# A selective-scan and mixture kernel: its first two and last two steps get their own order of stages and the PSUM banks of the scans

## What is computed

```
x = x + block(layernorm(x));  x = x + experts(layernorm(x))
block(x):   u = layernorm(x)*w + b; xm, z = split(u @ in_proj)
            xc = silu(conv4(xm) + b);  low, B, C = split(xc @ x_proj)
            dt = softplus(low @ dt_proj + b)
            for t: h = h*exp(dt*A) + dt*B*xc;  y = sum_s(h*C)   # 16 states s, 512 channels
            x1 = x + ((y + xc*D) * silu(z)) @ out_proj
            x2 = x1 + (silu(gate) * up) @ ff_out, gate and up from layernorm(x1) @ ff_proj
experts(x): weights of the best 2 of softmax(x/|x| @ router);  sum_e w_e * (x @ Wa[e] @ Wb[e])
```

## Time and profile before

| | |
|---|---|
| median of 3 runs | 1402.63 (1399.36 to 1402.98) |
| profiled execution | 1402.94, span 1401.2 |
| TensorE matmul busy | 1246.7, 89% of the span |
| TensorE weight load busy | 1064.7, 76% |
| VectorE busy | 971.9, 69% |
| ScalarE busy | 1058.5, 76% |
| GpSimd busy | 1092.9, 78% |
| chain that ended last | 71% TensorE, 10% ScalarE, 8% VectorE |

### The profile page before, as it was taken

How to read it: one execution, slowest core, us unless ns; L and a number is a source line. 1 busy time by engine, 2 the same in 40 slices (tenths; PEclk the granted TensorE clock), 3 DMA queues, 4 the chain that set the end, 5 groups by cost and what they waited for, 6 DMA issues and landing times.

```text
span 1401.2 us, 24298 instructions
## 1 busy us (share of the span) xinstructions
PE 1246.7 (89%) x7680; PEld 1064.7 (76%) x7680; DVE 971.9 (69%) x1765; ACT 1058.5 (76%) x2537; POOL 1092.9 (78%) x826
## 2 busy tenths in 40 slices
PE   4577888999999999999999999999999998999785
PEld 2255767788878888787878878887878877888663
DVE  2257777878686877878687777868687777877321
ACT  2489898878787988878787987878787887878110
POOL 2359899888889888888888888888888887887511
PEclk8588999999999999999999999999999999999898
DMA  2301111112111211112111211212011211111001
GB/s 76 138 31 47 39 46 39 60 47 76 46 62 31 84 39 45 64 47 76 48 54 39 76 47 33 76 47 76 33 67 39 76 39 31 69 46 62 19 33 40
DMA packets 29223, 75.08 MB, mean 54 GB/s; under 512 B 3104, under 2 KB 15776, under 8 KB 26528
## 3 DMA queue, kind: packets, MB, share of 16 engines
q1 hardware_dynamic: 29088, 73.41, 15.7%
HBM read 64.61 MB, written 4.59 MB: 49 GB/s over the span
## 4 chain that ended last, share of the span: by engine, by line
PE 71%; ACT 10%; DVE 8%; issue 6%; POOL 3%; DMA 2%; DVEq 0%; ACTq 0%; POOLq 0%; SPq 0%
PE psx L1109 12%; PE psy L1128 11%; PE psb L997 8%; PE psb L1003 8%; PE pst L1003 8%; PE pst L997 7%; PE psf L997 3%; DVE h L911 3%; ACT bxT L724 3%; ACT dA L736 3%; PE psf L1029 2%; PE psf L1079 2%; PE psf L1085 2%; DVE acc L887 2%; PE psf L1036 2%
## 5 line engine op out<-in xcount | busy, mean ns | idle before, releaser
L911 DVE TENSOR_TENSOR_SCAN h<-dA,state,psx 128x256 f32<-128x256 f32 x1024 | 681.7, 728 | 122.8 <-PE psx L1109 109.8
L518 POOL TENSOR_TENSOR hC<-h,bC 128x1024 f32<-128x1024 f32 x256 | 606.3, 2372 | 103.7 <-DVE h L911 81.6
L736 ACT ACTIVATE dA<-dt,neg_a 128x256 f32<-128x256 f32 x1024 | 434.3, 500 | 0.0
L1109 PE MATMUL psx<-ident,bxT 128*128 128x128 f32 x2048 | 307.8, 277 | 20.8 <-DVE h L911 14.0
L724 ACT ACTIVATE bxT<-uTs,BT 128x512 f32<-128x512 f32 x384 | 254.1, 717 | 67.9 <-PE psx L1109 66.2
L1109 PEld LDWEIGHTS psx<-ident,bxT 128*128 128x128 f32 x2048 | 246.8, 143 | 64.1 <-issue 26.6
L1128 PE MATMUL psy<-ident,hC 128*128 128x128 f32 x2048 | 267.0, 274 | 1.0 <-POOL hC L518 1.0
L1128 PEld LDWEIGHTS psy<-ident,hC 128*128 128x128 f32 x2048 | 234.7, 142 | 4.1 <-POOL hC L518 1.3
L997 PE MATMUL pst<-eT,w_a_sb 128*128 128x256 f32 x512 | 127.6, 394 | 22.8 <-DVE cbc L967 22.4
L502 POOL TENSOR_TENSOR bxT<-uTs,BT 128x1024 f32<-128x1024 f32 x64 | 121.6, 1900 | 32.6 <-PE psx L1109 32.6
L997 PE MATMUL psb<-nT,w_ff_sb 128*128 128x256 f32 x512 | 125.7, 388 | 13.3 <-ACT yg L749 12.4
(11 more groups left out here) (121 smaller groups left out, 1583.6 us busy)
## 6 DMA issues: line engine op xcount, KB each, us to landing
bC<-bc_scratch SPq DMA_DIRECT2D x64, 512.0 KB, 3.9
cbc<-cw_scratch SPq DMA_DIRECT2D x16, 1024.0 KB, 4.8
xf<-in_x SPq DMA_DIRECT2D x16, 256.0 KB, 2.7
xk<-xn SPq DMA_DIRECT2D x16, 256.0 KB, 4.3
xb<-in_x SPq DMA_DIRECT2D x16, 256.0 KB, 4.2
out<-x SPq DMA_DIRECT2D x16, 256.0 KB, 2.2
w_in_sb<-in_w_in SPq DMA_DIRECT2D x1, 1024.0 KB, 5.4
w_ff_sb<-in_w_ff SPq DMA_DIRECT2D x1, 1024.0 KB, 5.8
```

The lines of the kernel that those rows point to most:

```text
L518: nc.gpsimd.tensor_tensor(hC[:, s % RC], h[:, ring(s)], bC[:, g % RINGG, s % G:s % G + 1, :].to_broadcast([P, NJ, T]), ALU.mult).then_inc( ...
L736: last = nc.scalar.activation(dA[:, s % RA, j, :], dt[:, n[1], j, :], ACT.Exp, scale=neg_a[:, j, s:s + 1])
L911: last = nc.vector.tensor_tensor_scan(h[:, r, j, :], dA[:, s % RA, j, :], psx[bx_bank(fill)][:, k, :], state[:, b, j, s:s + 1], ALU.mult, ...
L1109: last = nc.tensor.transpose(psx[bx_bank(fill)][:, k, j * P:(j + 1) * P], bxT[:, ring(s), j, c:c + P], ident[:, :])
```

## The change

`drive` no longer runs the first two and the last two iterations; two lists, `opening()` and `closing()`, name the pieces in their order, the same for every engine. Some pieces of these steps use other banks, and waits that guarded the shared bank are left out or put elsewhere. For step (0, 0): `bc` and BT go to pst, z1 to psb, the turns of u to psy; x1 of (0, 0) and (0, 1) goes to psx[2]. The product `low` of (0, 0) now goes ahead of `bc`. The skip scaling of (0, 0) moves on ScalarE from ready 12 to enter 12 of (0, 1). For the last chunk wa0 to wa3 go to psx[0..2] and psf, all four ahead of VectorE's use; for (7, 1) they go directly behind the logits, ahead of cT, G1 and A0 go to psy, and wb runs expert by expert for both token halves, each behind its own quarter of VectorE's products. The steps between are as before.

```diff
+FIRST_IN_UNITS = ["uT", "x0", "x1", "low", "bc"]
+LAST_TAIL_UNITS = ["xeT", "rt", "wa0", "wa1", "wa2", "wa3", "cT", "wb"]
+def opening():
+    a, b = (0, 0), (0, 1)
+    def turns(stage, step, *at):
+        return [(stage, s, step) for s in at]
+    return (turns("enter", a, *range(11), 13, 14, 15) + turns("ready", a, 0, 1, 2) + turns("enter", a, 11, 12)
+            + turns("ready", a, 5, 6) + turns("enter", b, 0, 1, 2, 3) + turns("ready", a, 7, 8)
+            + turns("enter", b, 4) + turns("ready", a, 9) + turns("enter", b, 5) + turns("ready", a, 10)
+            + turns("enter", b, 6, 7, 8, 9, 10) + turns("ready", a, 12, 13, 14, 15)
+            + turns("enter", b, 11, 12, 13, 14, 15))
+def closing():
+    a, b = (NC - 1, 0), (NC - 1, 1)
...
+    return (turns("back", b, 0, 1) + turns("tail", a, 0, 1) + turns("back", b, 2, 3) + turns("tail", a, 2, 3)
+            + turns("back", b, 4) + turns("tail", a, 4, 5) + turns("back", b, 5, 6, 7)
+            + turns("tail", a, 6, 7, 8, 9, 10) + turns("back", b, 8, 9, 10, 11) + turns("tail", a, 12)
+            + turns("back", b, 12, 13, 14) + turns("tail", a, 13, 14, 15) + turns("back", b, 15)
+            + turns("tail", b, *range(S)))
-    iteration(None, None, None, None, (0, 0))
-    iteration(None, None, None, (0, 0), (0, 1))
+    for name, s, step in opening():
+        stages[name](s, step)
...
-    iteration((NC - 1, 0), (NC - 1, 1), None, None, None)
-    iteration((NC - 1, 1), None, None, None, None)
+    for name, s, step in closing():
+        stages[name](s, step)
+        def x_bank(i, m):
+            return psx[2] if i and is_early(m) else psf
+        def gate_bank(i, m):
+            return psy3(0) if i and is_last(m) else psb
+        def up_bank(i, m):
+            return psy3(1) if not i and is_last(m) else psb
+        def wa_bank(i, m):
+            return (psx[0], psx[1], psx[2], psf)[i] if is_late(m) else pst
```

`is_early` is true for chunk 0, `is_late` for chunk 7. On TensorE:

```diff
                 if s == 5:
-                    pe.wait_ge(conv_tap, count(NJ * (TAPS - 1), m, NJ // 2 * (TAPS - 1)))
-                    project(psf, w_in_sb, uT[:, b], KM, [2 * P, 3 * P]).then_inc(filled_in, 1)
+                    pe.wait_ge(conv_tap, count(NJ * (TAPS - 1), m, 0 if is_early(m) else NJ // 2 * (TAPS - 1)))
+                    project(x_bank(1, m), w_in_sb, uT[:, b], KM, [2 * P, 3 * P]).then_inc(filled_in, 1)
...
+                if is_first(n) and fill == 2:
+                    pe.wait_ge(conv_tap, 2 * NJ * (TAPS - 1))
...
+                    if not is_last(m):
+                        pe.wait_ge(gate_done, count(2, m, 1))
+                    project(gate_bank(1, m), w_ff_sb, nT, KM, [HID // 2 + 2 * P, HID // 2 + 3 * P]).then_inc(filled_back, 1)
+                    if not is_last(m):
+                        pe.wait_ge(gate_done, count(2, m, 2))
+                    project(up_bank(0, m), w_ff_sb, nT, KM, [0, P]).then_inc(filled_back, 1)
...
+                if s == 12 and is_last(m):
+                    pe.wait_ge(cT_done, count(1, m, 1))
+                    for e in range(NE):
+                        pe.wait_ge(hE_done, count(NE // 2, m, e // 2 + 1))
+                        for j in range(SUB):
+                            last = mm(pst[:, j, :], cbc[:, e, j * P:(j + 1) * P], w_b_sb[:, e, :],
+                                      start=e == 0 and j == 0, stop=e == NE - 1, skip_group_check=True)
+                    last.then_inc(filled_tail, 1)
...
+            def hidden(i, m):
+                first(m, "a")
+                if is_late(m):
+                    pe.wait_ge(hE_done, count(NE // 2, m, 0))
+                elif i == 0:
+                    pe.wait_ge(cT_done, count(1, m, 1))
+                else:
+                    pe.wait_ge(hE_done, count(NE // 2, m, i))
+                project(wa_bank(i, m), w_a_sb, eT, KM, [2 * i * RANK, (2 * i + 1) * RANK]).then_inc(filled_tail, 1)
```

More of the change, by code:

```diff
@@ L128, in pair @@
         iteration((c - 1, 1), (c, 0), (c, 1), (c + 1, 0), (c + 1, 1))
-    iteration(None, None, None, None, (0, 0))
-    iteration(None, None, None, (0, 0), (0, 1))
+    stages = {"enter": enter, "ready": ready, "back": back, "tail": tail}
+    for name, s, step in opening():
+        stages[name](s, step)
     iteration(None, None, (0, 0), (0, 1), (1, 0))
@@ L654, in enter @@
                     act.wait_ge(filled_in, in_fill("bc", m))
-                    nc.scalar.activation(bc[:, :], psf[0:2 * S, 1, :], ACT.Copy).then_inc(bc_done, 1)
+                    nc.scalar.activation(bc[:, :], (pst if is_first(m) else psf)[0:2 * S, 1, :], ACT.Copy
+                                         ).then_inc(bc_done, 1)
+                if s == 12 and is_early(m) and not is_first(m):
+                    skip(prev(m))
             def ready(s, m):
@@ L688, in ready @@
                     act.wait_ge(filled_dt, dt_fill("z1", m))
-                    nc.scalar.activation(sz[:, b, 1, :], psf[:, :, :].rearrange("p k t -> p (k t)"), ACT.Copy
+                    src = psb if is_first(m) else psf
+                    nc.scalar.activation(sz[:, b, 1, :], src[:, :, :].rearrange("p k t -> p (k t)"), ACT.Copy
                                          ).then_inc(z1_copied, 1)
[L691 to L697, removed]
+                if s == 12 and not is_first(m):
+                    skip(m)
                 if s in (13, 14):
@@ L703, in ready, with skip @@
                     act.wait_ge(filled_dt, dt_fill(f"UT{j}", m))
-                    nc.scalar.activation(uTs[:, b, j, :], psf[:, :, :].rearrange("p k t -> p (k t)"), ACT.Copy
-                                         ).then_inc(uTs_done, 1)
+                    src = psy[j][:, :] if is_first(m) else psf[:, :, :].rearrange("p k t -> p (k t)")
+                    nc.scalar.activation(uTs[:, b, j, :], src, ACT.Copy).then_inc(uTs_done, 1)
                 if s >= 13:
                     made(s - S, m)
+            def skip(m):
+                act.wait_ge(xc_done, count(1, m, 1 if is_last(m) else 2))
+                for j in range(NJ):
+                    last = nc.scalar.activation(sk[:, j, :], xc[:, m[1], j, :], ACT.Copy, scale=pcol(C_DSKIP + j))
+                last.then_inc(skip_ready, 1)
             def made(turn, n):
@@ L1207, in tail @@
                     last.then_inc(filled_tail, 1)
+                    if is_last(m):
+                        for i in range(NE // 2):
+                            hidden(i, m)
                 if s == 4:
```

97 lines of the change are left out of this document (56 added, 41 removed).

## The result

The changed kernel takes 1363.07 us (median of 4 runs, 1361.78 to 1364.54) against 1402.8 before (here the median of 4 runs): a ratio of 0.9718, 95% interval 0.9706 to 0.9731. It is 39.7 us faster; 32 were forecast. The profiled execution took 1364.54 for a span of 1362.8.

A forecast was written before the change was run, and what follows sets the result against it. At both ends one instruction is in flight at a time, through true dependences and removable waits for banks or queue places. Opening 15 plus closing 17 is 32; 1402.6 - 32 = 1370.6 us, range 1360 to 1384.

The forecast's parts named there:

- Opening, 15.0 forecast: First two steps: 17.3 us earlier at the first uTs copy, less 2.1 and 0.2, for everything from b's low copy on.
- Step 1: Opening: x1 of (0, 0) in psx[2] no longer waits for x0's taps, starts 3.7 us earlier; Silu starts at 22.9.
- Step 2: Opening: low goes ahead of bc, two step-size halves follow, the wait for bc costs some 2 us; Exp at 37.4.
- Step 3: Opening: Exp, Ln, correction and GpSimd's three passes make u ready at 48.7; xn of (0, 1) queues behind, to 51.1.
- Step 4: Opening: projections of (0, 1) at half clock; its Silu at 52.5, between 51.4 and 53.6; first uTs copy 17.3 us earlier.
- Step 5: Opening: skip scalings and b's bc copy, now behind the first uTs copy on ScalarE, give back 2.1 us.
- Closing, 17 forecast: Last two steps: 9.15 us up to the first product of cbc plus 7.9 behind it, 17.05 in all.
- Gain given back: Rival: the iteration behind the opening returns its gain, only a quarter of 15 left; 1382 us, chance 12%.
- Clock low at the end: Rival: last burst all at half clock, 5.3 us more, and b's expert-in products, 7.2 more; 1383 us, chance 10%.
- Denser ends get full clock: Rival: opening worth 18.4 and closing 20, 1364 us, or 1360 if low and bc also run at full clock; chance 12%.
- It does not do what it says: Rival for both ends: the last user of a shared bank is never the wait that ends last; 1402 us, chance 2%.
- Slower by the clock in the iterations behind: Rival: TensorE's clock in 80 to 200 falls from 0.90 to 0.50, 52 us more than the stretch; 1423 us, chance 3%.

The follow-up runs named there:

- last_tail_old: The changed kernel, but the tail of step (7, 1) alone runs as before the change; 1376.75 us.
- closing_old_order: The changed kernel with all its closing banks, but the last two iterations run in the old order of stages; 1369.07 us.
- opening_only: The changed kernel with its new opening list and banks, but the last two iterations put back as before the change; 1383.35 us.
- warm_last: The changed kernel plus fifteen matmuls without use behind the turn of cw in step (7, 1), into psy; 1361.52 us.
- warm_opening: The changed kernel plus ten matmuls without use behind x1 of (0, 0), into psb; 1362.58 us.
- x1_shared_bank: The changed kernel, but x1 of both first steps goes to shared bank psf again and waits for the taps of x0; 1373.71 us.
- after_again: The changed kernel itself, unaltered, run once more beside three other kernels on one chip; 1364.7 us.

## Why the prediction was right, and its sizes too small

The direction, the two places and the mechanisms were right. 1363.07 lies in the range of 1360 to 1384, and in the 1363 to 1378 of my own forecast only by its last 0.07. The gain was summed 7.7 too small: 4.9 in the opening, 1.6 in the closing, and 1.2 by which the medians differ more than the profiles. Point by point:

- **Opening, 15.0 forecast, 19.9 measured.** This is the term that was mis-sized, and the clock is what it mis-sized. Step 1: a's Silu was to start at 22.9 and started at 21.72, since x1 took 2.60 where I put 3.7. Step 2: Exp was to start at 37.4 and started at 35.00; another 1.2, of which `bc` (2.78 instead of 3.78) is 1.0. Step 3 was right in kind: GpSimd's chain with `xn` in it ended last, and took 14.2 from Exp to Silu, counted as 14.0 (37.4 to 51.4). Step 4: I took the middle between a rising clock and a low one, 52.5, with z1, x0 and x1 of b at 3.8 each. The clock rose, they took 1.88, 1.99 and 1.99, TensorE was done long before, and Silu started at 49.16, ahead of the 51 to 54 that I had named as a sign: 2.4 from the steps before it, 0.9 from the middle. Step 5, the 2.1 and 0.2 that come back on ScalarE, measured 1.9 (20.6 saved at the first uTs copy, 18.7 at the copy of b's `low`). So 18.7 is the measure of the term as it was defined. Another 1.2 came behind it, from a place that the sum did not have:

```profile
88.65 1.91 PE L1109 MATMUL psx<-ident,bxT 128*128 128x128 f32 x8
```

```profile
69.35 1.04 PE L1185 MATMUL psx<-ident,bxT 128*128 128x128 f32 x8
```

The same eight transposes took 1.91 before (first row) and 1.04 after (second row): before, TensorE was at half clock there, and ScalarE then waited 1.66 for the transposes of the next step; after, 0.34. At that point the changed kernel is 20.4 ahead, of which 0.5 is lost up to the first ygt. The bound of 11, that GpSimd does not catch up, did not come: its first hC starts 13.4 earlier (67.58 instead of 80.96), the first ygt 19.9.
- **Closing, 17 forecast, 18.6 measured.** To xeT of b 11.1 was saved where I had 9.5: the second half of the out projection took 1.89 where I had left the 2.85 of before, and gate and up products, expert-out and ff-out followed as counted. The 9.04 from xeT to the turn of cw became 9.31. The last step was right: 10.2 from the first cbc product (9.95 forecast), with a burst of 9.38. My arithmetic there was loose: 9 x 0.45 + 23 x 0.22 is 9.1, not 9.2, and 8 x 3.78 / 2 is 15.1, not 14.5; with the rows' own durations (3.78 / 8 and 7.17 / 32) nine cold matmuls give 9.4. That it was nine I had guessed, so the match is in part luck: the burst took 9.16 to 10.02 in the nine profiles that have it without a filler. `last_tail_old` puts this part at 8.7, `closing_old_order` the order at 5.4; the forecast had not told order and banks apart.
- **The rivals.** Gain given back: false, `opening_only` keeps 19.8 to the first ygt. Clock low at the end: the last burst did start cold, for 2.2 us, as the sum had it, and `warm_last` shows that price; the expert-in products of b ran at full clock. Denser ends get full clock, 1364 at 12%: the time that came is this rival's, and for the dense stretch from 33 on so is the cause (x1 of b at 1.99). But its parts were 18.4 and 20, measured 19.9 and 18.6: it had the last burst at full clock, which was cold, and Silu of b at 51.4, so its total is met by errors that cancel. `warm_opening` shows what the clock is worth on this chain at `low`, which stayed at half clock in the changed kernel. It does not do what it says: false, `x1_shared_bank` and the rows of both ends. Slower by the clock in the iterations behind: false, 0.91 in 60 to 165.
- The Trainium skill, TensorE: Matmul & The Clock Gate, "HAM oscillation — how this bites in real kernels", was weighed as speaking against the change. `warm_last` agrees that a burst behind a wait pays (9.38 against 7.14). But the same rule speaks for the change in the opening, which I did not see: the banks close the waits between bursts, and `x1_shared_bank` shows the fall of the clock when one is opened again (1.99 for x0 of b, then a wait of 3.48, then 3.55).

The middle took 1158.3 to 1164.1 with the same code in all of these profiles. In two pairs of profiles I followed the ygt marks through it. Against `warm_last` the changed kernel's first profile loses 2.2 us up to the third step's ygt (at 288.22) and 0.1 in all behind it; `after_again` loses 3.0 against it behind the last ygt but one (at 1230.45). TensorE's clock was granted differently in just these parts: in the stretch from 220 to 260 it is 0.96 in the changed kernel's first profile (middle 1160.6) and 1.00 in that of `warm_last` (1158.3); from 1220 to 1260 it is 0.96 in the first profile and 0.91 in that of `after_again` (1163.0):

```profile
220.00:260.00 40.00, 37.95 (x218) 0.96 0.20 67
1220.00:1260.00 40.00, 35.77 (x250) 0.96 0.19 67
```

```profile
220.00:260.00 40.00, 38.09 (x234) 1.00 0.20 67
```

```profile
1220.00:1260.00 40.00, 34.06 (x235) 0.91 0.18 67
```

(length, busy us of TensorE, granted clock, DMA share, GB/s; after, `warm_last`, `after_again`.) What stays open is why the clock is granted differently there, and whether it accounts for all of the difference. Also open: `x1_shared_bank` gives 9.1 of the opening's 19.9 to one bank; how the rest divides between the order of the stages, `low` ahead of `bc`, and the banks of `bc`, z1, BT and the turns of u, no run tells.

## What to carry to other kernels

Where a pipeline fills and drains, the buffers of the stage that is idle are free: one PSUM bank more for the second projection was worth 9 us here, since it removed the two waits and TensorE's clock didn't fall in them. A stage that is moved ahead on all engines alike moves in each queue past other things: look for the one piece that now stands ahead of the last link (`xn` on GpSimd, 2.5 us; `bc` on ScalarE, 1.4). When a sum has matmuls at half clock, ask which of them will be adjacent after the change, rather than taking over their old durations.

## What the runs showed of the hardware

The granted clock of the first 15 us can't be read from the records, so the 0.70 and 0.81 of the first windows are both a little high: the kernel before shows 1.00 in its window from 12 to 14, but x0 took 3.75 for its eight matmuls there, twice the 1.9 to 2.0 of the same group at full clock (busy us, granted clock, DMA share, GB/s):

```profile
12.00:14.00 2.00, 2.00 (x6) 1.00 0.46 131
```

Between executions of code that is the same up to there the clock rose at different places of the same chain (1.10 or 2.05 for the first step-size product of a, in the profiles of the changed kernel and of `last_tail_old`; 1.99 or 3.67 for the first half of the last out projection, in two profiles of the changed kernel). Exp of a moved by 1.8 us with it (34.68 to 36.46) and the opening by 3 (135.3 to 138.3), as much as the small edits. A filler of matmuls that ends before the next real one may start showed no cost and took 1.8 us off `low` and 2.2 off the final burst.
